# Seeding half of the score banks of a latent attention core from ScalarE in place of TensorE

## The reference

```python
q, k, v = heads(latents @ Wq), heads(cat(ctx, latents) @ Wk), heads(cat(ctx, latents) @ Wv)
weights = softmax(q @ k.T / 8)        # per batch and head: 512 x 1536
out = (weights @ v) @ Wout
```

## Time and profile before

| what | value |
|---|---|
| median of three runs | 4804.18 us |
| profiled execution, its own time | 4800.99 us |
| its span (first to last instruction) | 4799.2 us |
| share of the span busy: PE, DVE, ACT, POOL | 86%, 60%, 49%, 28% |
| mean granted TensorE clock, share of full | 0.914 |
| the stage of the change, first to last product | about 2719 to 3634 us |

### The profile page before, as it was taken

The page is one execution under the profiler, slowest core; times in us unless marked ns, Lnnn a source line. Parts: engine busy times, 40 slices in busy tenths (PEclk is TensorE's granted clock), DMA queues, the critical chain, the costliest instruction groups (busy, mean ns, idle before and its releaser), DMA issues. The chain is left out here.

```text
span 4799.2 us, 67609 instructions
## 1 busy us (share of the span) xinstructions
PE 4132.2 (86%) x20384; PEld 1961.2 (41%) x20384; DVE 2871.1 (60%) x6517; ACT 2346.1 (49%) x4572; POOL 1359.8 (28%) x1202
## 2 busy tenths in 40 slices
PE   8789755698789996897989999999998989489886
PEld 6322444395552233573234333333335644222224
DVE  4668484202658884004862488888873256488876
ACT  4447240243245774333654455555542246189992
POOL 0122050112111111112120288787882213000112
PEclk9879877799888998898999999999998999699998
DMA  8654202454043222674335511122111044623411
GB/s 291 145 113 115 73 1 36 186 184 142 9 144 69 60 54 72 244 243 149 71 94 192 182 62 62 63 68 72 62 45 39 7 122 99 150 66 94 98 38 39
DMA packets 332035, 486.47 MB, mean 101 GB/s; under 512 B 84516, under 2 KB 232596, under 8 KB 317252
## 3 DMA queue, kind: packets, MB, share of 16 engines
q1 hardware_dynamic: 321552, 443.63, 32.3%
q0 software_dynamic: 6384, 32.61, 2.1%
q10 hardware_dynamic: 3804, 6.74, 0.4%
HBM read 327.63 MB, written 143.92 MB: 98 GB/s over the span
## 5 line engine op out<-in xcount | busy, mean ns | idle before, releaser
L1432 POOL TENSOR_TENSOR lc_totals<-lc_totals,lc_weights 128x1024 f32<-128x1024 f32 (+1 forms) x320 | 623.7, 1949 | 163.4 <-DVE lc_totals L1381 134.1
L1341 ACT ACTIVATE lc_weights<-ps 128x1024 f32<-128x1024 f32 x384 | 393.0, 1024 | 402.1 <-PE ps L1227 391.6
L1362 DVE TENSOR_REDUCE lc_part_max<-ps 128x2 f32<-128x1024 f32 x384 | 466.1, 1214 | 205.1 <-PE ps L1207 201.5
L1227 PE MATMUL ps<-lc_q,lc_k 64*128 64x512 f32 x1536 | 392.3, 589 | 0.0
L1237 PE MATMUL ps<-lc_weights,lc_v 128*64 128x512 f32 x1536 | 371.7, 605 | 0.0
L898 DVE TENSOR_REDUCE l1x_core_part_max<-ps 128x1 f32<-128x512 f32 x512 | 318.8, 682 | 67.8 <-PE ps L719 66.9
L894 DVE CUSTOM_DVE_ANT_0 l3x_core_unused<-ps,l3x_core_mask_q 128x512 f32<-128x512 f32 x512 | 334.1, 686 | 8.2 <-DVE l3x_core_row_max L902 3.9
L857 ACT ACTIVATE l3x_core_weights<-ps 128x512 f32<-128x512 f32 x512 | 315.7, 663 | 20.2 <-PE ps L786 15.4
L857 ACT ACTIVATE l1x_core_weights<-ps 128x512 f32<-128x512 f32 x512 | 266.7, 603 | 93.6 <-PE ps L786 93.5
L840 ACT ACTIVATE ps<-l3x_core_mask_k 128x512 f32<-128x512 f32 x384 | 258.8, 674 | 36.1 <-DMA l3x_core_mask_k<-in_mask_k 36.1
L719 PE MATMUL ps<-l3x_core_k,l3x_core_q 96*128 96x512 bf16 x512 | 211.6, 414 | 51.5 <-DVE l3x_core_part_max L894 33.2
(11 more groups left out here) (494 smaller groups left out, 8526.1 us busy)
## 6 DMA issues: line engine op xcount, KB each, us to landing
cf_w<-in_L1f_w SPq DMA_DIRECT2D x32, 1024.0 KB, 7.7
lc_k<-latent_k SPq DMA_DIRECT2D x32, 768.0 KB
lc_v<-latent_values SPq DMA_DIRECT2D x32, 768.0 KB, 5.0
latent_k<-feed_staged SPq DMA_DIRECT2D x64, 256.0 KB, 2.6
latent_values<-feed_staged SPq DMA_DIRECT2D x64, 256.0 KB, 2.0
k_heads<-proj_parts SPq DMA_DIRECT2D x40, 384.0 KB, 2.6
q_heads<-proj_parts SPq DMA_DIRECT2D x32, 384.0 KB, 2.6
q_heads<-proj_parts SPq DMA_DIRECT2D x32, 256.0 KB, 3.0
```

The costliest lines, as they stand in the source:

```text
L1227: mm = nc.tensor.matmul(out[j], k_tile[g % RING][strip(j), i * P:(i + 1) * P], q_tile[g % RING][strip(j), :], start=False, stop=True)
L1341: nc.scalar.activation(weights[:, i % TILES, :, :], k.ps[:, B0 + (i % 2) * HEADS:B0 + (i % 2 + 1) * HEADS, 0:nq], ACT.Exp, scale=scale).th ...
L1362: nc.vector.reduce_max(own, k.ps[:, A0:A0 + HEADS, :], AX).then_inc(a_taken, 1)
L1432: nc.gpsimd.tensor_tensor(total, total, own, ALU.add).then_inc(added_by_pool, 1)
```

## The change

For even key tiles the bf16 product of ones and `max_row` is dropped. Instead ACT copies a float32 broadcast of the negated maxima, `tops` (128 partitions by 1024), into the two banks (`fill`), and the key-query product is added to that. To make `tops`, DVE joins the two bf16 parts into a float32 row (`joined`), SP stores it to device memory (`max_rows`) and loads it back broadcast to all partitions. For odd tiles nothing changes, but the wait for `max_row` moves to tile 1. A fill stands in ACT's list behind the `Exp` of the even tile two before it; that of the following group's tile 0 stands behind the `Exp` of tile 10. ACT's rounding is split into the queries behind tile 3 and two halves of the keys behind tiles 5 and 7. Before the first group TensorE multiplies once into the even tiles' banks (`opened`). SP's list of groups is written out where it was a loop.

```diff
+    def by_scalar(i):
+        return i % 2 == 0
+    FILLS = nkt // 2
...
+        joined, tops = sb("joined", [SLOTS, P]), sb("tops", [P, 2, HEADS, nq])
+        max_rows = nc.dram_tensor("lc_max_rows", [2, SLOTS, P], F32, kind="Internal").ap()
...   # SP: row(b, g)
-                sync.wait_ge(row_made, at(b, g, 1, 1))
+                sync.wait_ge(parts_joined, at(b, g, 1, 1))
+                sync.dma_start(max_rows[g % 2, :, :], joined[:, :]).then_inc(tops_out, 16)
                 for j in range(HEADS):
                     for p in range(ROW_PARTS):
                         sync.dma_start(max_row[...], max_parts[...]).then_inc(row_in, 16)
+                if not before(b, g, 2):
+                    sync.wait_ge(filled, at(b, g, FILLS, -FILLS))
+                sync.wait_ge(tops_out, 16 * at(b, g, 1, 1))
+                sync.dma_start(tops[:, g % 2, :, :].rearrange("p j n -> p (j n)"),
+                               max_rows[g % 2, :, :].rearrange("s t -> (s t)").partition_broadcast(P)).then_inc(tops_in, 16)
...
-            for_groups(sync, group)
+            for_groups(sync, group, turns=0)
...   # TensorE: scores(b, g, i)
                 if i == 0:
                     pe.wait_ge(loaded[g % RING], loads_done(b, g))
+                if i == 1:
                     pe.wait_ge(row_in, 16 * HEADS * ROW_PARTS * at(b, g, 1, 1))
+                if by_scalar(i):
+                    pe.wait_ge(filled, at(b, g, FILLS, i // 2 + 1))
+                else:
+                    if not (before(b, g, 1) and i < 2):
+                        pe.wait_ge(exp_done, at(b, g, nkt, i - 1))
+                    for j in range(HEADS):
+                        nc.tensor.matmul(out[j], ones_row[strip(j), :], max_row[strip(j), g % 2, :], start=True, stop=False)
                 for j in range(HEADS):
-                    nc.tensor.matmul(out[j], ones_row[strip(j), :], max_row[strip(j), g % 2, :], start=True, stop=False)
-                for j in range(HEADS):
-                    mm = nc.tensor.matmul(out[j], k_tile..., q_tile..., start=False, stop=True)
+                    mm = nc.tensor.matmul(out[j], k_tile..., q_tile..., start=False, stop=not by_scalar(i), skip_group_check=by_scalar(i))
...   # ACT
+            def fill(b, g, i):
+                if i == 0:
+                    act.wait_ge(tops_in, 16 * at(b, g, 1, 1))
+                if not (before(b, g, 1) and i == 0):
+                    act.wait_ge(exp_done, at(b, g, nkt, i - 1))
+                nc.scalar.activation(k.ps[:, B0:B0 + HEADS, 0:nq], tops[:, g % 2, :, :], ACT.Copy).then_inc(filled, 1)
...   # ACT: group(b, g), behind the Exp of tile i
+                    if by_scalar(i) and i + 2 < nkt:
+                        fill(b, g, i + 2)
+                    elif by_scalar(i) and exists(*later(b, g, 1)):
+                        fill(*later(b, g, 1), 0)
...
-                    if i == 5 and exists(*later(b, g, 2)):
-                        round_operands(*later(b, g, 2))
+                    if i in (3, 5, 7) and exists(*later(b, g, 2)):
+                        round_operands(*later(b, g, 2), [(i - 3) // 2])
...   # DVE: end of negate(b, g)
+                dve.wait_ge(row_made, at(b, g, 1, 1))
+                if not before(b, g, 1):
+                    dve.wait_ge(tops_out, 16 * at(b, g, 1, 0))
+                nc.vector.tensor_tensor(joined[:, :], max_parts[:, 0, :], max_parts[:, 1, :], ALU.add).then_inc(parts_joined, 1)
```

More of the change, by code:

```diff
@@ L1103, in latent_core_stage @@
         negative, max_parts = sb("negative", [SLOTS, P]), sb("max_parts", [SLOTS, ROW_PARTS, P], BF16)
+        joined, tops = sb("joined", [SLOTS, P]), sb("tops", [P, 2, HEADS, nq])
+        max_rows = nc.dram_tensor("lc_max_rows", [2, SLOTS, P], F32, kind="Internal").ap()
         (rounded, a_ready, a_taken, row_done, turned, high_made, row_made, row_in, s_ready, exp_done, pv_done, acc_copied,
-         added_by_pool, added_by_vector, sums_ready, inverted, normed, set_up, left_ready, left_taken, *more) = held.enter_context(k.stage(
+         added_by_pool, added_by_vector, sums_ready, inverted, normed, set_up, left_ready, left_taken,
+         parts_joined, tops_out, tops_in, opened, filled, *more) = held.enter_context(k.stage(
              "rounded", "a_ready", "a_taken", "row_done", "turned", "high_made", "row_made", "row_in", "s_ready", "exp_done", "pv_done",
-             "acc_copied", "added_by_pool", "added_by_vector", "sums_ready", "inverted", "normed", "set_up", "left_ready", "left_taken",
+             "acc_copied", "added_by_pool", "added_by_vector", "sums_ready", "inverted", "normed", "set_up", "left_ready", "left_taken", "parts_joined", "tops_out", "tops_in", "opened", "filled",
              *(f"left_stored{i}" for i in range(len(left) // LEFT_BANKS)), *(f"loaded{r}" for r in range(RING)), *(f"v_loaded{r}" for r in range(V_RING))))
@@ L1201, in pass_a @@
                 if p == 0:
-                    pe.wait_ge(rounded, at(b, g, 2, 2))
+                    pe.wait_ge(rounded, at(b, g, 3, 3))
                 if not (before(b, g, 1) and p == 0):
@@ L1219, in scores @@
                     pe.wait_ge(loaded[g % RING], loads_done(b, g))
+                if i == 1:
                     pe.wait_ge(row_in, 16 * HEADS * ROW_PARTS * at(b, g, 1, 1))
-                if not (before(b, g, 1) and i < 2):
-                    pe.wait_ge(exp_done, at(b, g, nkt, i - 1))
                 out = [k.ps[:, B0 + (i % 2) * HEADS + j, 0:nq] for j in range(HEADS)]
+                if by_scalar(i):
[5 more added lines that the diff above has]
+                        nc.tensor.matmul(out[j], ones_row[strip(j), :], max_row[strip(j), g % 2, :], start=True, stop=False)
                 for j in range(HEADS):
-                    nc.tensor.matmul(out[j], ones_row[strip(j), :], max_row[strip(j), g % 2, :], start=True, stop=False)
-                for j in range(HEADS):
-                    mm = nc.tensor.matmul(out[j], k_tile[g % RING][strip(j), i * P:(i + 1) * P], q_tile[g % RING][strip(j), :], start=False, stop=True)
+                    mm = nc.tensor.matmul(out[j], k_tile[g % RING][strip(j), i * P:(i + 1) * P], q_tile[g % RING][strip(j), :], start=False,
+                                          stop=not by_scalar(i), skip_group_check=by_scalar(i))
                 mm.then_inc(s_ready, 1)
@@ L1271, in _ @@
                 pe.wait_ge(left_taken, len(left))
+            pe.wait_ge(loaded[0], loads_done(0, 0))
+            for j in range(HEADS):
+                nc.tensor.matmul(k.ps[:, B0 + j, 0:nq], k_tile[0][strip(j), 0:P], q_tile[0][strip(j), :], start=True, stop=False,
+                                 skip_group_check=True).then_inc(opened, 1)
             def group(b, g):
@@ L1300, in _, with round_operands @@
         def _(act):
[L1301 to L1306, removed]
+            def round_operands(b, g, some=range(3)):
+                for part in some:
+                    if part == 0:
+                        act.wait_ge(loaded[g % RING], loads_done(b, g))
+                        if not before(b, g, 2):
+                            act.wait_ge(a_ready, at(b, g, NP, -NP))
+                        nc.scalar.activation(q_round[:, g % 2, :], q_tile[g % RING][:], ACT.Copy).then_inc(rounded, 1)
+                    else:
+                        own = slice((part - 1) * nk // 2, part * nk // 2)
+                        nc.scalar.activation(k_round[:, g % 2, own], k_tile[g % RING][:, own], ACT.Copy).then_inc(rounded, 1)
+            def fill(b, g, i):
[4 more added lines that the diff above has]
+                nc.scalar.activation(k.ps[:, B0:B0 + HEADS, 0:nq], tops[:, g % 2, :, :], ACT.Copy).then_inc(filled, 1)
             def copy_sums(b, g):
@@ L1331, in _ @@
                 act.wait_ge(stored, 16 * LEFT_BANKS)
+            act.wait_ge(opened, HEADS)
+            fill(0, 0, 0)
             def group(b, g):
```

## The result

The changed kernel takes 4993.37 us in the median of four runs (4987.99 to 5016.51), the kernel before 4803.04 on the same chips (4801.34 to 4805.68): a ratio of 1.0405, with an interval of 1.0371 to 1.0439. It is slower by some 190 us. The forecast was 5010, in a range from 4925 to 5090. The profiled execution has a span of 4986.2 us.

A forecast was written before the change was run, and what follows sets the result against it. TensorE's list was taken to set the pace at 28.38 us a group; 20.45 + 2.2 + 12.44 = 35.09, 6.71 more, 208 us over 31 groups, plus 1 us in the first, gave 5010 us, range 4925 to 5090.

The forecast's parts named there:

- What is removed: TensorE's bf16 product pairs for even tiles, six per group at 0.215 us: 41 us at most over 192 pairs.
- fills, rounding and lists beside TensorE: Inside a group, ACT's fills and split rounding and SP's written-out list were to cost nothing, hidden beside TensorE's 4.34 us pair.
- The fill of the first group: One ACT fill ahead of the first group's scores, claimed to cost 1 us.
- The path to the fill: Turn to end of the next group's tile 0 fill: 12.44 us, TensorE ready at 6.64, a 5.8 us wait in 31 groups.
- parts: The negated bf16 parts of the maxima, said to be written 2.43 us behind the turn.
- join: DVE's added operation on the two parts, expected to end 1.3 us later, behind a POOL operation (bounds 0.3 and 2.0).
- DMAs ahead of the broadcast: SP issues five, the joined row's store and the four old ones, at 0.65 us each with the fifth: 3.13 us.
- landing: The broadcast from issue to landing, taken as 4.4 us from norm-row loads of the same size and shape.
- The clock: Behind each group's wait TensorE's clock falls to 0.50; half of 4.4 us is lost, 2.2 us per group.
- Rival one: The wait for the broadcast comes but TensorE's clock does not fall: 33.09 us a group, 4948 us; chance 0.15.
- Rival two: The broadcast lands in time for tile 0's fill; 0.56 us a group stays saved, 4783 us; chance 0.04.
- the chain of sums: POOL and DVE additions waiting for each other up to TensorE's product 11; with a timely broadcast, gives back 0.73 us a group.

The follow-up runs named there:

- the second experiment: The changed kernel with the broadcast read from a constant input at the head of the row routine, waiting for neither turn nor join: 4805.67 us, ratio 1.0004.

## Why the prediction came out

The groups' lengths make a ladder, each step with the runs that show it:

| step | us a group | shown by |
|---|---|---|
| before | 28.38 | |
| products of even tiles gone | -1.29 | 6 x 0.215 |
| product 8 waits for DVE's list | +0.41 | no wait, no join: 27.52 |
| join ahead of a reduction | +0.88 | with the join: 28.40 |
| wait for the broadcast | +4.2 | turn to scores 7.53 without it, 11.72 after |
| lower clock behind the wait | +1.6 to 1.9 | products in the wait: 20.99 for 22.57 |
| after: sum of the steps | 34.2 to 34.5 | measured 34.28, mean 34.64 |

**What is removed** was right: a pair inside a group takes 4.34 us, as said (in the group shown its scores start at 3418.20 and those of the next pair at 3422.54). But the claim that fills, rounding and lists beside TensorE cost nothing was right for ACT and SP only. DVE was looked at for the length of its join and not for what stands behind it. There the saving of 1.29 meets two first-pass products that need DVE, and DVE has no room: 0.4 at product 8, 0.88 at product 10. In the changed kernel the second lies inside the wait and shows in no total, which is why the forecast could miss it. Without the wait it decides the result. The fill of the first group, set at 1 us, held TensorE for 3.54, behind ACT's wait for earlier stores.

**The path to the fill**, term by term, in the group shown: parts 2.65 for 2.43, join 1.28 for 1.3, DMAs ahead of the broadcast 2.88 for 3.13, landing with its waking 3.71 for 4.4 and a part of 0.13, fill 1.03 for 1.05, and 0.14 to the scores. The sum is 11.69 for 12.44, and over all groups 11.72. The term that was mis-sized is the landing: 3.7 us in the median, where 4.4 had been taken from the loads of norm rows. The price that the Trainium skill gives in DMA: Bandwidth & Descriptors, section Anatomy of one DMA, 3.2 us as an estimate for this size, was 0.5 too low; the shortest landing here was 3.3.

**The clock** fell as said, at the start of every group. Behind the 31 waits the stretches at 0.50 last 3.4 us in 26 groups and 6.8 in the other five, where 4.4 had been taken as the mean of the three in the earlier trace rows, and the cost is 1.6 to 1.9 us for 2.2. The granted clock of the stage is 0.94, where about 0.9 had been said. The Trainium skill tells in TensorE: Matmul & The Clock Gate, section HAM oscillation, of a loop that waits for a DMA in each turn and starts each turn at the lower clock; this trace agrees, with 0.50 behind each of the 31 waits. Rival one, in which the clock stays, would have needed 4948: the run in which it was made to stay took 4951.67.

**How near, and by what.** A group was to take 35.09 us and takes 34.28. The place of the cost, the path and the fall of the clock are as forecast. That the total came within 17 us is in part luck: the path was 0.7 too long and the clock's cost 0.3 to 0.6 too high, while 0.41 at product 8 and some 2.5 us in the first group had been left out, and these errors have opposite signs.

**The rivals.** Rival two, the broadcast in time, gave 4783. With the broadcast made timely the kernel took 4805.67, and 4789.53 without the join. The second is near the rival's number, but the reason given was wrong: the chain of sums was to hold back 0.73 a group behind product 3, and three kernels with the normalisation moved show no change. What held was DVE's order at products 8 and 10. The chain did move along with TensorE, by way of POOL: in the kernel without the join, DVE's addition of tile 8 started before POOL's operation on that tile and took 0.67 us, not 1.7. That the chain can bind is shown by the later addition of tile 5.

**Left open:** why the low stretch is twice as long behind five of the 31 waits. From turn to turn the first group, those five and five that stand next to them take 35.2 to 38.0 us and all others 34.6 at most, which is why the mean (34.64) lies above the median; no run shows what makes them.

## What to carry to other kernels

When an operand is moved from one engine to another, price the path on which it becomes ready (here turn, parts, join, five DMAs, landing, fill: 11.7 us) against the slack of its earliest user (7.5), and not the operation that it replaces (0.215 us a pair). Where the saving is about a microsecond a turn on the engine that sets the pace, look through the list of the next engine for every small operation put ahead of something that the first one waits for; a 1.15 us join on DVE ate what was left of the gain. A late first use can be given back to the old way: filling only tiles whose data are surely there, and storing the row as it is, turned +190 us into -7 (-2 to -12).

## What the runs showed of the hardware

In these traces a DVE operation with two SBUF operands that starts while POOL is in an operation ends only behind it. The join takes 0.28 us in the one group where POOL is idle, and 1.14 to 1.37 in the other 31, where it ends 0.14 to 0.15 us behind the POOL operation beside it in every case (3399.35 behind 3399.19 above). In the kernel before, POOL starts first on tile 8 and DVE's addition is stretched:

```profile
3142.91 1.71 DVE L1381 TENSOR_TENSOR lc_totals<-lc_totals,lc_weights 128x512 f32<-128x512 f32 x1
...
3142.80 1.27 POOL L1432 TENSOR_TENSOR lc_totals<-lc_totals,lc_weights 128x512 f32<-128x512 f32 x1
```

Without the join DVE came 0.02 us ahead of POOL (3135.54 and 3135.56), took 0.67, and POOL's took 1.78. The Trainium skill, SBUF — State Buffer, section Who interferes with whom, says that DVE and GpSimd share a pair of ports under an exclusive lock; these two pairs of rows agree with it. DVE's start, 0.11 us behind POOL's in one pair and 0.02 ahead of it in the other, moves 1.04 us off DVE's operation and 0.51 onto POOL's, which was not expected.

A copy of 128x1024 float32 from SBUF into PSUM took ACT 1.03 us in every one of 192 cases, the same as the Exp of that size out of PSUM (1.02). The load of the 4 KB row to all partitions, 512 KB, from device memory to which it had just been stored, landed 3.7 us from its issue in the median (3.3 to 4.7), where the loads of norm rows have 4.4 (4.1 to 4.8). In the second experiment the broadcast of a constant of the same size, issued right behind the group's loads of values, queries and keys, took longer; the list of its tile has:

```profile
DMA to landing us min/median/max: 5.9/7.9/15.6
```
